# Context values of a decoder's last layer: computed in the first cross attention instead of beside the routing, with a turned tile copied last in ScalarE's step

## The reference

```python
def _L0_xattn_ref(x, cond, wq, bq, wkv, bkv, wp, bp):
    q = _qdq(x) @ _qdq(wq).T + bq
    kv = cond @ wkv.T + bkv
    attn = softmax(einsum('bnhd,bmhd->bhnm', q, k) * scale)
    out = _qdq(einsum('bhnm,bmhd->bnhd', attn, v)) @ _qdq(wp).T + bp
...
# layer 1's attention over the context and the tokens, 4 key heads of 128
k_ctx = rope(rms_norm(context @ Wk.T), context_position_ids)
v_ctx = context @ Wv.T
```

## Time and profile before

| | us |
|---|---|
| median of three runs | 2729.94 |
| the profiled execution | 2728.3 |
| its span in the trace | 2726.6 |
| PE busy | 2479.4 (91%) |
| DVE busy | 1704.5 (63%) |
| ACT busy | 1154.6 (42%) |
| POOL busy | 934.5 (34%) |
| granted PE clock, mean | 0.951 of full |

### The profile page before, as it was taken

The page is one execution under the profiler, slowest core; times in us unless marked ns, Lnnn a source line. Parts: engine busy times, 40 slices in busy tenths (PEclk is TensorE's granted clock), DMA queues, the critical chain, the costliest instruction groups (busy, mean ns, idle before and its releaser), DMA issues. The chain is left out here.

```text
span 2726.6 us, 48715 instructions
## 1 busy us (share of the span) xinstructions
PE 2479.4 (91%) x14967; PEld 2033.7 (75%) x14968; DVE 1704.5 (63%) x3211; ACT 1154.6 (42%) x2389; POOL 934.5 (34%) x943
## 2 busy tenths in 40 slices
PE   7999788879899999799997998997999998999998
PEld 7888666658688887588875886665777787888887
DVE  4536847769777666676675566866555535666564
ACT  2103256623343334455553233757655522444443
POOL 4203201134333234423333212753333312355554
PEclk9999989989899989899998988998999989999999
DMA  5544122125622055477774432444222131666664
GB/s 191 154 140 114 28 93 77 46 91 168 179 68 65 15 166 182 147 220 223 195 223 105 131 68 96 151 125 126 73 70 72 55 129 63 182 163 159 147 163 73
DMA packets 304547, 336.59 MB, mean 123 GB/s; under 512 B 149231, under 2 KB 220063, under 8 KB 302578
## 3 DMA queue, kind: packets, MB, share of 16 engines
q1 hardware_dynamic: 233170, 256.24, 30.1%
q0 software_dynamic: 20640, 51.74, 9.7%
q10 hardware_dynamic: 50560, 26.34, 3.3%
HBM read 235.70 MB, written 98.56 MB: 123 GB/s over the span
## 5 line engine op out<-in xcount | busy, mean ns | idle before, releaser
L898 PE MATMUL e_psum<-e_up_hi,hT_hi 128*128 x672 | 244.9, 365 | 14.5 <-DVE hT_lo L867 11.0
L900 PE MATMUL e_psum<-e_up_hi,hT_lo 128*128 x672 | 237.0, 353 | 0.0
L899 PE MATMUL e_psum<-e_up_lo,hT_hi 128*128 x672 | 236.4, 352 | 0.0
L1938 POOL TENSOR_TENSOR joint_a_p<-joint_a_p,joint_a_rinv 112x487 f32<-112x487 f32 x128 | 125.5, 1002 | 187.5 <-DVE joint_a_rinv L1992 187.1
L1569 POOL TENSOR_TENSOR self_a_p<-self_a_p,self_a_mx 112x448 f32<-112x448 f32 x96 | 96.1, 1002 | 205.8 <-DVE self_a_mx L1626 205.8
L898 PEld LDWEIGHTS e_psum<-e_up_hi,hT_hi 128*128 128x128 f32 x672 | 127.6, 190 | 34.7 <-issue 24.5
L794 ACT ACTIVATE e_gate<-e_psum 128x352 f32<-128x352 f32 (+1 forms) x86 | 44.5, 517 | 247.0 <-PE e_psum L900 246.6
L1997 DVE TENSOR_REDUCE joint_a_mx<-joint_psum 112x1 f32<-112x487 f32 x128 | 84.9, 663 | 101.4 <-PE joint_psum L1963 100.7
L873 DVE TENSOR_TENSOR hT_lo<-e_psum,hT_hi 128x256 fp32r<-128x256 f32 (+2 forms) x138 | 55.7, 435 | 144.8 <-ACT hT_hi L812 144.8
L1660 ACT ACTIVATE self_a_p<-self_a_p 112x448 f32<-112x448 f32 x128 | 71.6, 574 | 168.1 <-POOL self_a_p L1569 114.9
L1211 POOL TENSOR_TENSOR p_p_z<-p_p_straight,p_p_crossed 128x512 f32<-128x512 f32 x70 | 98.4, 1407 | 112.5 <-DVE p_p_crossed L1193 110.5
(11 more groups left out here) (574 smaller groups left out, 7483.0 us busy)
## 6 DMA issues: line engine op xcount, KB each, us to landing
e_up_raw<-in_L_ffn_w SPq DMA_DIRECT2D x64, 512.0 KB, 5.0
e_up_raw<-in_L_ffn_w SPq DMA_DIRECT2D x64, 352.0 KB, 4.1
e_dn_raw<-in_L_ffn_w SPq DMA_DIRECT2D x16, 1024.0 KB, 5.5
q_all<-p_p_t_stage ACTq DMA_DIRECT2D x56, 256.0 KB, 2.3
e_dn_raw<-in_L_ffn_w SPq DMA_DIRECT2D x16, 512.0 KB, 6.3
x_first<-q_all SPq DMA_DIRECT2D x32, 224.0 KB, 2.7
v_ctx<-front_c_v_stage SPq DMA_DIRECT2D x24, 250.0 KB
x_others<-k_ctx SPq DMA_DIRECT2D x8, 750.0 KB, 5.3
```

The lines of the kernel that those rows point to most:

```text
L898: pe.matmul(out, lhs[0], rhs[0], start=k == 0, stop=False)
L899: pe.matmul(out, lhs[0], rhs[1], start=False, stop=False)
L900: return pe.matmul(out, lhs[1], rhs[0], start=False, stop=k == n_k - 1)
L1938: pool.tensor_tensor(p[:, r, 0:S], p[:, r, 0:S], rinv[:, r:r + 1].to_broadcast([T, S]), ALU.mult).then_inc(p_ready, 1)
```

## The change

1. `ContextRopePart` makes only keys. Its value products, the value copies on DVE and their stores are gone, and so is Wv's load and split. The keys have four PSUM banks instead of three. In ACT's step the copy and the store of the turned tile come last.
2. A new `ContextValuesPart` "v" makes the 24 value tiles in the first cross attention. Each item loads 125 columns of the transposed context (250 KB in runs of 500 bytes) into one buffer, ACT makes the high part, POOL the low part, PE multiplies in two halves of 6 matmuls in bank 7, DVE copies, SP stores to a tensor of its own, `v_ctx4`, which the joint attention reads.
3. The weight Wv is split by a new part "fv" at the stage's start; "f" uses its buffer behind it.
4. Bank 7 is now shared: the two turns of `OutNormPart` wait for value copies (`others_in_bank`), and the value products for `OutNormPart`'s readers (`bank_free`). Nine items are placed in the first steps, fifteen between the steps of `OutNormPart`.
5. `RopeQkvPart`: in ACT's step the turned tile is copied last too. In the projection without a norm there is nothing between the two places.
6. `CrossAttentionPart` keeps two result tiles instead of four (`O_RING`).

```diff
@@ RopeQkvPart, scalar @@
-                i = step - LR
-                if 0 <= i < n_rot:
...
-                    act.activation(t_stage[:, i % 3, :, :], src, ACT.Copy).then_inc(t_ready, 1)
...
                 if eps is not None and step < n_rot:
...
                     last.then_inc(z_ready, 1)
+                i = step - LR
+                if 0 <= i < n_rot:
...
+                    act.activation(t_stage[:, i % 3, :, :], src, ACT.Copy).then_inc(t_ready, 1)
...
@@ CrossAttentionPart @@
-        N_S, N_T, O_RING = len(s_banks), len(t_banks), 4
+        N_S, N_T, O_RING = len(s_banks), len(t_banks), 2
@@ OutNormPart, tensor @@
                         pe.wait_ge(h_ready, m + 1)
+                        if others_in_bank:
+                            others_in_bank(pe, 2 * b + 1)
...
                         reuse(pe, ht_ready, turned)
+                        if others_in_bank:
+                            others_in_bank(pe, 2 * b)
@@ ContextRopePart @@
-                for v in values_at(i - 1):
-                    sp.wait_ge(v_ready, v + 1)
-                    sp.dma_start(v_to[v // CCH, v % CCH, 0:CT, :], v_stage[:, v % 2, :]).then_inc(v_stored[v % 2], 16)
...
-                for v in values_at(i):
-                    dve.wait_ge(v_mm, v + 1)
-                    reuse(dve, v_stored[v % 2], 16 * (v // 2))
-                    dve.tensor_copy(v_stage[:, v % 2, :], ps[0:CT, v_banks[v % len(v_banks)], :]).then_inc(v_ready, 1)
...
-                for m in values_at(i):
...
-                    products(pe, ps[0:CT, v_banks[m % len(v_banks)], :], lambda k: (c_hi[:, u, k, tok(n)], c_lo[:, u, k, tok(n)]),
-                             lambda k: (w_hi[:, 1, k, :], w_lo[:, 1, k, :]), KC).then_inc(v_mm, 1)
@@ new: ContextValuesPart @@
+            def load(i):
+                b, n = i // CCH, i % CCH
+                reuse(sp, c_ready, i)
+                sp.dma_start(c_raw[:, :, 0:CT], core.ins["ctxT"][b][:, :, n * CT:(n + 1) * CT]).then_inc(c_in, 16)
...
+                pool.tensor_tensor(c_lo[:, i % 2, :, :], c_raw[:, :, :], c_hi[:, i % 2, :, :].bitcast(F32), ALU.subtract).then_inc(c_ready, 1)
...
+                act.wait_ge(c_in, 16 * (i + 1))
+                reuse(act, v_mm, i - 1)
+                act.activation(c_hi[:, i % 2, :, :], c_raw[:, :, :], ACT.Copy).then_inc(c_hi_ready, 1)
...
+                pe.wait_ge(c_ready, i + 1)
+                reuse(pe, v_ready, i)
+                bank_free(pe, i)
+                for k in range(KC):
+                    pe.matmul(out, c_hi[:, u, k, 0:CT], w_hi[:, k, :], start=(k == 0), stop=False)
+                    pe.matmul(out, c_hi[:, u, k, 0:CT], w_lo[:, k, :], start=False, stop=False)
+                    last = pe.matmul(out, c_lo[:, u, k, 0:CT], w_hi[:, k, :], start=False, stop=(k == KC - 1))
+                    if k == KC // 2 - 1:
+                        yield
@@ decoder, the first cross attention @@
-                    order = attention_order(a, o, 8, 8, gap=0.95)
-                    g.run(["landed"] + order[:90] + ["f"] + order[90:130] + [n for name in order[130:138] for n in (name, "f")] + order[138:])
+                                    others_in_bank=lambda pe, n: pe.wait_ge(v.v_ready, at_start + n))
+                    fv = FirstWeightPart(g, "fv", ins["L1_xattn_Wv"], wq, wv_lo)
+                    f = FirstWeightPart(g, "f", ins["L0_ffn_wq"][0], first_hi, first_lo, behind=fv)
+                    def bank_free(pe, i):
+                        n = i - at_start
+                        if n >= 0:
+                            pe.wait_ge(o.ht_ready if n % 2 else o.added, n // 2 + 1)
...
+                    g.run(["landed", "fv"] + beside_context_values(attention_order(a, o, 8, 8, gap=0.95), at_start))
@@ decoder, the routing @@
-                    c = ContextRopePart(g, "c", "L1_xattn_Wk", "L1_xattn_Wv", k_ctx, v_ctx, ctx_tabs, 1e-6, (0, 1, 2), (3, 4), (5, 6), last_context)
+                    c = ContextRopePart(g, "c", "L1_xattn_Wk", k_ctx, ctx_tabs, 1e-6, (0, 1, 2, 3), (5, 6), last_context)
```

More of the change, by code:

```diff
@@ L2677, in tensor, with __init__, sync, gpsimd @@
                     last.then_inc(z_used, 1)
+                yield
+        g.part(name, sync=sync, gpsimd=gpsimd, scalar=scalar, vector=vector, tensor=tensor)
+class ContextValuesPart:
+    def __init__(self, g, name, w_hi, w_lo, w_ready, v_to, bank, bank_free, v_stage):
+        core, ps = g.core, g.ps
+        n_items, CP = B * CCH, CT + CT % 2
+        c_raw = g.sb(f"{name}_c_raw", [128, KC, CP])
+        c_hi = g.sb(f"{name}_c_hi", [128, 2, KC, CP], F32R)
+        c_lo = g.sb(f"{name}_c_lo", [128, 2, KC, CP], F32R)
+        c_in, padded, c_hi_ready, c_ready, v_mm, self.v_ready = (g.sem(f"{name}_{n}") for n in ("c_in", "padded", "c_hi_ready", "c_ready", "v_mm", "v_ready"))
+        v_stored = g.sems(f"{name}_v_stored", 2)
+        v_ready = self.v_ready
+        self.steps = 2 + 3 * n_items
+        def sync(sp):
+            def load(i):
+                b, n = i // CCH, i % CCH
+                reuse(sp, c_ready, i)
+                sp.dma_start(c_raw[:, :, 0:CT], core.ins["ctxT"][b][:, :, n * CT:(n + 1) * CT]).then_inc(c_in, 16)
+            sp.wait_ge(padded, 1)
+            load(0)
+            yield
+            load(1)
+            yield
+            for i in range(n_items):
+                yield
+                yield
+                if i + 2 < n_items:
+                    load(i + 2)
+                sp.wait_ge(v_ready, i + 1)
+                sp.dma_start(v_to[i // CCH, i % CCH, 0:CT, :], v_stage[:, i % 2, :]).then_inc(v_stored[i % 2], 16)
+                yield
+            for u in range(2):
+                sp.wait_ge(v_stored[u], 8 * n_items)
+        def gpsimd(pool):
+            def split_low(i):
+                pool.wait_ge(c_hi_ready, i + 1)
+                pool.tensor_tensor(c_lo[:, i % 2, :, :], c_raw[:, :, :], c_hi[:, i % 2, :, :].bitcast(F32), ALU.subtract).then_inc(c_ready, 1)
+            pool.memset(c_raw[:, :, CT:CP], 0.0).then_inc(padded, 1)
+            yield
+            split_low(0)
+            yield
+            for i in range(n_items):
+                yield
+                if i + 1 < n_items:
+                    split_low(i + 1)
+                yield
+                yield
+        def scalar(act):
+            def split_high(i):
+                act.wait_ge(c_in, 16 * (i + 1))
+                reuse(act, v_mm, i - 1)
+                act.activation(c_hi[:, i % 2, :, :], c_raw[:, :, :], ACT.Copy).then_inc(c_hi_ready, 1)
+            yield
+            split_high(0)
+            yield
+            for i in range(n_items):
+                yield
+                if i + 1 < n_items:
+                    split_high(i + 1)
+                yield
+                yield
+        def vector(dve):
+            yield
+            yield
+            for i in range(n_items):
+                yield
+                yield
+                dve.wait_ge(v_mm, i + 1)
+                reuse(dve, v_stored[i % 2], 16 * (i // 2))
+                dve.tensor_copy(v_stage[:, i % 2, :], ps[0:CT, bank, :]).then_inc(v_ready, 1)
+                yield
+        def tensor(pe):
+            yield
+            yield
+            for i in range(n_items):
+                u, out = i % 2, ps[0:CT, bank, :]
+                if i == 0:
+                    pe.wait_ge(w_ready, KC)
+                pe.wait_ge(c_ready, i + 1)
+                reuse(pe, v_ready, i)
+                bank_free(pe, i)
+                for k in range(KC):
+                    pe.matmul(out, c_hi[:, u, k, 0:CT], w_hi[:, k, :], start=(k == 0), stop=False)
+                    pe.matmul(out, c_hi[:, u, k, 0:CT], w_lo[:, k, :], start=False, stop=False)
+                    last = pe.matmul(out, c_lo[:, u, k, 0:CT], w_hi[:, k, :], start=False, stop=(k == KC - 1))
+                    if k == KC // 2 - 1:
+                        yield
+                last.then_inc(v_mm, 1)
+                yield
@@ L2881, in sync @@
         def sync(sp):
+            if behind:
+                sp.wait_ge(behind.ready, KC)
             for c in range(KC):
@@ L3451, in attention_order, with beside_context_values @@
     return order + extra + ["o"] * (n_o - done_o)
+def beside_context_values(order, at_start):
+    done_a, done_o, placed, at = -2, -1, [], {}
+    half = 4
+    for n in range(at_start):
+        first, second, third = (half, half, half + 1) if n < 2 * at_start - 14 else (half, half + 1, half + 2)
+        for h in (first, second, third):
+            at.setdefault(("a", h), []).append("v")
+        half = third
+    for b in range(B):
+        for start in (8 * b + 4,) + (8 * b + 8,) * (b + 1 < B):
+            at.setdefault(("o", start), []).append("v")
+            at.setdefault(("o", start + 1), []).append("v")
+            at.setdefault(("a", start + 18) if start + 18 <= order.count("a") - 2 else ("o", start + 1), []).append("v")
+    for name in order:
+        placed.append(name)
+        if name == "a":
```

(13 more changed lines are left out.)

121 lines of the change are left out of this document (54 added, 67 removed).

## The result

The changed kernel takes 2745.93 us, the median of five runs (2743.5 to 2747.79), against 2731.29 for the kernel before in the same comparison (2729.03 to 2733.78). The ratio is 1.0058, with a 95% interval of 1.0045 to 1.0071: slower, by 14.6 us between the medians. Its profiled execution has a span of 2745.1 us against 2726.6.

The account below looks back on a forecast made before the run. PE was taken to bound the stage beside the routing (170.41 of 185.00 us busy), with 54.5 us idle in the cross attention. 45.5 - 29 - 11 = +5.5 on 2728.3, the median 1.6 higher, gave 2735; range 2705 to 2756.

Parts of the forecast that it names:

- Part 2: Cross attention's start, up to the tenth scores: longer by +24 us, ends +15 and +38.
- The third rival: Cross attention's start: context loads over 5.5 us set the pace, price 38 instead of 24; kernel around 2750, chance 0.12.
- Part 3: Cross attention's middle: two items added a batch, +2.9 us each, +17 over 5.9 batches, ends +11 and +28.
- The steps A to D: Four steps of a middle cross-attention batch: 5.86, 5.38, 7.19, 4.95 us before; forecast 7.3, 6.0, 8.5, 5.9.
- Part 4: Cross attention's tail: one value tile and its copy ahead of the last turns, +4.5 us, ends +1 and +7.
- Part 5: Stage beside the routing: PE's item falls, the key tile's chain binds at 4.37 us; -29, ends -45 and -22.
- Part 6: Projection with a norm: copy last cuts ACT's loop, 3.61 to 3.21 us a tile; -11, ends -13 and 0.
- At nothing: Terms charged zero: two result tiles, "f" behind "fv", value stores in the cross attention, SP's waits for value copies.
- The lock: DVE and GpSimd's shared ports: 24 low parts could cost DVE up to 27 us in the cross attention; sum left unchanged.

## Why the prediction was right or wrong

**The time and the side.** 2735 was forecast with slower as the likelier sign; it is 2745.93, inside the range. The rise is nearly three times what I had, 14.6 for 5.5, and the place where it arose is the one named, the cross attention. But that the time lies within 11 us of the forecast is in part luck: the cross attention grew by 67.1 for 45.5, past the end of 60 that I had given it, and of the 21.6 us too little there 12.6 are balanced by the other two stages, which gained 10.5 and 2.1 more than forecast. The cross attention below is cut as in the prediction, at the tenth scores and at the turn of the rounded tile (before at 546.99, after at 610.15): +32.8, +27.4 and +7.0.

**Part 2, the start: +24 forecast, +32.8 measured, within its ends (15 to 38) but wrong in its working.** I put PE's 15 us first and let the loads "mostly hide" behind it at 2. The three runs on products and loads show that taking the products away alone gives 0.5 us, the loads alone 1.8, and both 19.1: they stand side by side, and while one is there the other's going saves next to nothing. The weight I had at 7 before the first exponentials, and it was 9 (11.4 less 2.3): the third chunk can't be issued before the first is split, which I had written down, and I had the landing of the second cover it. It doesn't: the first two are issued together and ACT splits the second at 360.60, one microsecond behind the first; the third, issued at 360.95, lands at 364.01, and ACT waits 2.78 us for it. The third rival, loads that land late, was half right; its condition, a load of over 5.5 us, did not come: the loads in their 500-byte runs land after 3.4 us in the median, those of the weight's 2 KB rows after 3.6, so their form made them no slower; the chain through one buffer is simply as long as PE's work. The Trainium skill, DMA: Bandwidth & Descriptors, Specifications, wants at least 512 bytes for full rate; at 250 KB a transfer, in this stage, these two rows show no penalty just below it.

**Part 3, the middle: +2.9 a batch forecast, +4.1 measured** in the three batches with a full clock and +4.7 in the mean of five; in all +27.4 for +17, just inside the end of 28. That the half ahead of L1761 lengthens the chain behind it was right: moving it gives 1.3 us a batch at full clock, and 2.8 where the clock fell. The steps A to D were forecast at 7.3, 6.0, 8.5 and 5.9 us and take 7.75, 6.74, 8.16 and 6.13. What I missed: B has its half item at full price (5.38 before, 6.74 now), where I let over half of it hide; a half item costs 1.54 us up to the next scores and not 1.39; and the waits for bank 7 (1.68 for h's split, 0.29 for the addition) took the place of the 2.30 us that I let the products fill. At a full clock PE is idle for 23.38 - 19.41 = 4.0 us of a batch before and for 28.82 - 25.32 = 3.5 after: of the 3.8 us of room that I counted, 0.5 was used. The clock, 0.92 before and full in three batches of five after, gives 1.3 back in those three (24.7 less 23.4); against a batch of before at the same clock they are 5.4 us longer, nearly all of the 5.6 us of work.

**Part 4, the tail: +4.5 forecast, +7.0 measured**, at its end of 7. Two value tiles stand ahead of turns here, and not one: at 614.47 ahead of the last L1761, +2.5 us to that turn, and at 625.45 ahead of the turn of the last rounded tile, another +2.6. The last stretch, from that turn to the addition, is 1.3 us longer, though PE's eight output products ran faster than before (2.1 us for 3.5), since the addition stands 3.2 us behind the low part of "f".

**Part 5, the routing: -29 forecast, -39.5 measured.** The item by ACT's chain was 4.37 forecast and is 4.23. The gain before deductions was 39, and the 10 us that I took back for late loads and for the clock were not seen: the clock did fall, to 0.84 from 0.92, but by the turns above PE waits for ACT's scaling and no longer sets the pace, and a slow PE is then mostly hidden (argued, as no run has this stage at a full clock). I charged PE's clock to a stage that I had just said PE doesn't bound. And PE was not the bound before that I took it for: 8 of the 39.5 us belong to the copy alone, with all the products still there, where I had some 4 for it.

**Part 6: -11 forecast, -13.1 measured**, 3.61 to 3.21 an item as worked out; the weight splits that I took back don't cost.

**At nothing.** One term was not nothing: the part "f" behind "fv". I wrote that its last chunks come in the tail as now. They don't: SP issues the third when DVE has made the low part of the first, which starts at 630.54 behind a value copy (before at 562.39, behind none), and the chunk takes 4.8 us from its issue at 631.25 to 636.07, where it took 3.0 before. DVE's addition, with two norms behind it, waits for that. It is worth 3.2 us at most; no run moves it. The profile shows nothing against the other terms, and the stages between and behind are within 1.4 us.

**The lock.** By the Trainium skill, SBUF — State Buffer, Who interferes with whom, the low parts on POOL could block DVE. The traces agree with it. L2295, whose inputs are both in SBUF, ends 0.55 us after the POOL instruction that began just before it, in three kernels: now the low part ends at 482.21 and L2295 at 482.76; before, L2176, which reads two tiles in SBUF, ended at 414.35 and L2295 at 414.90; with the half item moved it is the low part at 475.96 and L2295 at 476.51. So it takes 1.73, 1.75 and 1.24 us, by when it starts. In the tail L2248 takes 1.39 us beside the last low part (at 626.84), and 0.43 each of the other seven times. In the middle the low part thus costs DVE no more than before only because it took the place of L2176.

## What to carry to other kernels

Idle time of an engine, summed over a stage, is not room. It is room only where ready work can stand in it without being ahead of the chain that ends the wait, and without a resource (here a PSUM bank) that the chain holds. Count it by the gap that a piece of work would stand in, as long as the piece, and charge the rest at full price: here 5.6 us of products lengthened a batch of the middle by 5.4 at the same clock, though 4.0 us of it had been idle. (That the whole stage grew by 67 us, as much as 24 x 2.78, is chance: the start grew by the weight and the loads too, and two moves in the order gave 18 back with all the products in place.)

When two things run beside each other, take both away before saying that neither matters. And where a part is said to change nothing, as "f" was here, look in the new profile for what waits for it. Run the small parts of a change alone: two moved blocks gave 24 us, and the large part cost 39 (24.3 and 14.6).

## What was not expected of the hardware

Three batches in a row ran at a full granted clock (1.00, 2.4 GHz) in the changed kernel, where before that happened in one of five, and the mean clock of the middle was 0.92. PE was kept busy through the place where it had waited 2.30 us. The clock thus paid 1.3 us a batch for the added work, the mean of before (24.7) less its full-clock batch (23.4). With one product a value tile the same five batches had 0.91 again, so it is the added work that kept the clock. I had not expected it to be that much.
